# A decoder layer on one core: where the third expert weight piece lands, and which engine normalises the last layer norm's rows

## The reference

```python
x = x + _L0_attn_ref(_layernorm(x, axis=-1), Wq, Wk, Wv, Wo, betas)            # segmented attention with a memory, 16 heads
x = x + _L0_xattn_ref(_layernorm(x, axis=-1), ctx_512, Wq, Wkv_expand, Wout)   # cross attention, 16 heads of 16
x = x + _L0_ffn_ref(_layernorm(x, axis=-1), gate, w0, w1, wo)                  # 8 experts, the best 2 of each token

def _layernorm(x, axis=-1, eps=1e-05):
    m = jnp.mean(x, axis=axis, keepdims=True)
    v = jnp.var(x, axis=axis, keepdims=True)
    return (x - m) / jnp.sqrt(v + eps)
```

## Time and profile before

| | us |
|---|---|
| median of three executions | 536.52 (533.1 to 539.55) |
| the profiled execution's own time | 537.06 |
| its span, first to last instruction | 534.8 |
| attention, to the barrier | about 303 |
| cross attention | about 88 |
| experts and the end | about 144 |

### The profile page before, as it was taken

The page is one execution under the profiler, slowest core; times in us unless marked ns, Lnnn a source line. Parts: engine busy times, 40 slices in busy tenths (PEclk is TensorE's granted clock), DMA queues, the critical chain, the costliest instruction groups (busy, mean ns, idle before and its releaser), DMA issues. The chain is left out here.

```text
span 534.8 us, 11854 instructions
## 1 busy us (share of the span) xinstructions
PE 491.5 (92%) x4181; PEld 418.1 (78%) x4190; DVE 343.3 (64%) x743; ACT 318.4 (60%) x759; POOL 134.3 (25%) x150
## 2 busy tenths in 40 slices
PE   8899999999999999999999879999849999999970
PEld 3778888888898888888779857777637888888860
DVE  6666666667644676666558465678674667666754
ACT  4677777778526777777673267898313444544430
POOL 5710000012100000000000189996122433443220
PEclk9999999999999999999999997999859999999995
DMA  9521111211100112210000243441044555554527
GB/s 263 182 61 60 59 59 59 59 54 46 29 31 21 45 57 59 59 59 20 1 1 2 68 131 119 130 149 42 1 157 150 153 162 174 164 143 165 167 69 245
DMA packets 25043, 49.10 MB, mean 92 GB/s; under 512 B 2977, under 2 KB 12210, under 8 KB 25010
## 3 DMA queue, kind: packets, MB, share of 16 engines
q1 hardware_dynamic: 20434, 40.65, 25.0%
q0 software_dynamic: 2240, 6.04, 3.3%
q10 hardware_dynamic: 2336, 1.97, 1.2%
HBM read 42.48 MB, written 6.16 MB: 91 GB/s over the span
## 5 line engine op out<-in xcount | busy, mean ns | idle before, releaser
L717 PE MATMUL psum<-a_xt_hi,a_qk_hi 128*128 128x512 f32 x128 | 53.7, 420 | 0.9 <-POOL a_qk_lo L325 0.9
L629 DVE COPY a_weights_t<-psum 64x256 f32<-64x256 f32 x32 | 13.7, 428 | 60.7 <-PE psum L834 60.7
L717 PE MATMUL psum<-a_xt_hi,a_qk_lo 128*128 128x512 f32 x128 | 50.1, 392 | 0.0
L1066 ACT ACTIVATE x_probs<-psum,x_neg_max 128x128 f32<-128x128 f32 x128 | 45.8, 401 | 7.1 <-DVE x_neg_max L1124 7.1
L717 PE MATMUL psum<-a_xt_lo,a_qk_hi 128*128 128x512 f32 x128 | 50.0, 390 | 0.0
L1558 ACT ACTIVATE e_inner_hi<-psum 128x512 fp32r<-128x512 f32 x23 | 13.8, 598 | 56.4 <-PE psum L1734 56.4
L1002 POOL MEMSET x_v_pad<- 128x1024 f32 x1 | 1.0, 952 | 167.5 <-POOLq L262 167.5
L1723 PE MATMUL psum<-expert_w_hi,e_x_hi 128*128 x92 | 38.4, 418 | 1.2 <-ACT e_x_hi L1538 1.2
L1515 POOL DMA_INDIRECT picks_dram<-x_wout,e_pick_row x23 | 22.7, 987 | 62.6 <-DVE x_wout L1671 62.6
L1663 DVE TENSOR_TENSOR e_inner_lo<-psum,e_inner_hi 128x512 fp32r<-128x512 f32 x23 | 15.9, 692 | 34.6 <-ACT e_inner_hi L1558 34.6
L848 PE MATMUL psum<-a_weights_t,a_v 64*128 64x64 f32 x256 | 34.9, 276 | 3.5 <-issue 2.6
(11 more groups left out here) (235 smaller groups left out, 1497.6 us busy)
## 6 DMA issues: line engine op xcount, KB each, us to landing
x_k_t<-in_expert_wo SPq DMA_DIRECT2D x23, 512.0 KB, 3.8
a_qk_raw<-in_wqk SPq DMA_DIRECT2D x32, 256.0 KB, 2.6
x_xn_t<-in_expert_w SPq DMA_DIRECT2D x13, 512.0 KB, 3.8
a_wv_raw<-in_wv SPq DMA_DIRECT2D x17, 256.0 KB, 2.8
xn_dram<-xn SPq DMA_DIRECT2D x2, 1024.0 KB
x_probs_t<-in_expert_w SPq DMA_DIRECT2D x3, 512.0 KB, 3.8
x_sb<-in_x SPq DMA_DIRECT2D x2, 512.0 KB, 4.8
x_k_t<-in_wo SPq DMA_DIRECT2D x1, 1024.0 KB, 10.4
```

Source lines behind the costliest of these rows:

```text
L717: last = pe.matmul(out, pick_l(left[a], k), pick_r(right[b], k), start=start and n == 0, stop=n == 3 * KD - 1, skip_group_check=not start)
L1066: last = act.activation(probs[:, ch, place, :], s_ps[ch][:, place, :], ACT.Exp, bias=neg_max[:, ch, place:place + 1], accum_out=sums[:, b ...
```

## The change

Two things change in `cross_phase`.

First, EARLY goes from 3 to 2, and `xn_t` is laid out by halves of the query columns: half 0 holds both row blocks of the first 512 columns (pairs 0 and 1), half 1 the others. A raw piece lands in one half. Piece 2 goes to half 0 as soon as pairs 0 and 1 are projected (`q_done` = 2), piece 3 to half 1 when all four are (`q_done` = 4), and from piece 4 on a piece is requested when the one two before it is split. The first two copies of `copy_weights` wait for piece 0 (u = 0) and piece 1 (u = 1) only.

Second, the rows of the third layer norm of batches 0 to 6 are made by POOL behind piece 15, not by DVE; batch 7 stays on DVE. POOL's first `root_of` moves behind piece 15 too. Each row instruction on POOL waits for the scores that still read its part of `xn`.

```diff
-EARLY = 3
+EARLY = 2
-    xn_t = sb("x_xn_t", [P, KD, B * S], F32)
+    xn_t = sb("x_xn_t", [P, HALVES, KD, BANK], F32)
...
-                if n == EARLY:
-                    sp.wait_ge(q_done, B // 2)
-                if 2 <= n < EARLY or n >= EARLY + 2:
+                if n in (EARLY, EARLY + 1):
+                    sp.wait_ge(q_done, 2 * (n - EARLY + 1))
+                if n >= EARLY + 2:
                     sp.wait_ge(w_split, n - 1)
...
+            def layernorm(b):
+                if b <= HB:
+                    pool.wait_ge(rstd3_ready, with_deviation[b])
+
+                pool.wait_ge(s_done, min(2 * (2 * b + 2), 2 * B))
+                pool.tensor_scalar(c.xn[:, b, :], c.x_sb[:, b, :], c.meanvar[:, b, 0:1], c.rstd[:, b:b + 1],
+                                   ALU.subtract, ALU.mult).then_inc(xn3_ready, 1)
+
             for n in range(PIECES):
-                if n == PIECES - 1:
-                    root_of(0)
...
+            root_of(0)
+            for b in range(HB):
+                layernorm(b)
             root_of(1)
+            for b in range(HB, B - 1):
+                layernorm(b)
             root_of(2)
...
                 if u < 2:
-                    act.wait_ge(w_split, EARLY)
+                    act.wait_ge(w_split, u + 1)
...
-                    if b == B - 1:
-                        layernorm(0)
-                        layernorm(1)
...
-                if b == B - 1:
-                    layernorm(2)
...
                 if u < 2:
-                    dve.wait_ge(w_split, EARLY)
+                    dve.wait_ge(w_split, u + 1)
...
-            layernorm(3)
...
-            layernorm(4)
-            layernorm(5)
...
-            layernorm(6)
```

More of the change, by code:

```diff
@@ L965, in raw_piece @@
             return probs_t[:, n % 2, :, :].rearrange("p h t -> p (h t)")
-        return xn_t[:, n % 2, :]
+        return xn_t[:, n % 2, :, :].rearrange("p k t -> p (k t)")
     def piece_loaded(n):
@@ L1042, in _ @@
                     act.wait_ge(xt_done, 1)
-                act.activation(xn_t[:, 0, half * BANK:(half + 1) * BANK], c.bank[half * KD][:, :], ACT.Copy).then_inc(xt_low_ready, 1)
+                act.activation(xn_t[:, half, 0, :], c.bank[half * KD][:, :], ACT.Copy).then_inc(xt_low_ready, 1)
             act.wait_ge(consts, c.n_x_consts)
@@ L1103, in _ @@
                     dve.wait_ge(xt_done, 2)
-                dve.tensor_copy(xn_t[:, 1, half * BANK:(half + 1) * BANK], c.bank[half * KD + 1][:, :]).then_inc(xt_high_ready, 1)
+                dve.tensor_copy(xn_t[:, half, 1, :], c.bank[half * KD + 1][:, :]).then_inc(xt_high_ready, 1)
             dve.wait_ge(consts, c.n_x_consts)
@@ L1193, in layernorm @@
                 dve.wait_ge(rstd3_ready, with_deviation[b])
+                dve.wait_ge(xn3_ready, b)
                 dve.tensor_scalar(c.xn[:, b, :], c.x_sb[:, b, :], c.meanvar[:, b, 0:1], c.rstd[:, b:b + 1],
@@ L1245, in project_queries @@
                     for k in range(KD):
-                        last = pe.matmul(q_banks(pair)[i], wq[:, k, i * P:(i + 1) * P], xn_t[:, k, pair_tokens(pair)],
-                                         start=k == 0, stop=k == KD - 1)
+                        last = pe.matmul(q_banks(pair)[i], wq[:, k, i * P:(i + 1) * P],
+                                         xn_t[:, pair // 2, k, pair % 2 * 2 * S:(pair % 2 + 1) * 2 * S], start=k == 0, stop=k == KD - 1)
                 last.then_inc(q_done, 1)
```

## The result

The changed kernel took 533.9 us in the median (22 executions), the kernel before 539.3 beside it; the ratio is 0.994 (95%: 0.9914 to 0.9967). The medians are of all executions, and the ratio leaves out the slow ones of both kernels (four of these 22, one of them of 2606 us), so it isn't 533.9 / 539.3. In a second comparison the changed kernel took 533.88 us, and the ratio was 0.9921 (0.9881 to 0.9961). In microseconds of some 537 that is a gain of 3.2 (1.8 to 4.6) and 4.2 (2.1 to 6.4), where the prediction forecast 5.5 by its sum. So the gain is clear of noise and smaller than forecast; the median lies inside the range, 2.3 us above the forecast, and under 1% of gain was the case held likeliest.

What follows compares the result with a forecast made beforehand. The prediction took the start as bound by ACT's wait for POOL's subtraction and PE's slow clock behind it, the middle by ACT. Sum: 537.06 - 1.6 - 3.4 - 0.5 = 531.6 us, range 529.5 to 533.5.

Steps and rivals of the forecast that it cites:

- the case held likeliest: Whole execution: a time within about 1% (5.4 us) of the kernel before, given 0.59; faster 0.32, slower 0.09.
- The stall and the clock: Start of cross attention: ACT's copy of chunk 0 no longer waits 2.44 us for POOL, and PE's clock holds at 1.00.
- Both terms, 1.6 and 3.4 us: Chunk 2 starts 1.6 us sooner; chunk 2 to chunk 4 takes 7.67 us instead of 11.05 at full clock, 3.4 us.
- The rival that the clock falls all the same: At PE's short gap or in the scores and weighing after it: the 3.4 us are missing, 535.0 us; chance 0.11.
- Where POOL stands: Near the end of the pieces: POOL's first root, behind piece 15, ends at about 367.3 us.
- slack of 1.7 us: POOL's five waits for PE to have weighed a batch, 1.7 us in all, which were to vanish.
- The price of a row: One layer norm row instruction on POOL: 0.6 us taken by size, between 0.40 and 2.4 us.
- bound of 1.0 us: POOL's rows near the end: hidden from PE up to about 1.0 us an instruction.
- all are hidden: At 0.6 us each, POOL's rows 0 to 6 are done before PE asks for them, costing nothing.
- late-rows rival: Near the end: at 2.4 us a row on POOL, PE waits and the gain is lost, 538.2 us; chance 0.35.
- What DVE gains: Between reciprocal and last copy: without its rows there, DVE's copy comes sooner for PE's weighing of batch 7, 0.5 us.
- the third rival: Clock also holds near the end: weighing and four transposes gain 1.5 us more, 530.1 us; counted within the forecast's 0.52.

Runs made afterwards that it cites:

- filling the stall: Kernel before with 11 unread 128x256 matmuls added on PE behind chunk 2's scores, ACT's wait kept: 535.18 us, ratio 0.9956.
- the half rows: Changed kernel with POOL's seven row instructions over 128 columns instead of 256: 532.76 us, ratio 0.9907 to the kernel before.
- the epsilon version: Changed kernel with the epsilon of batches 0 to 3 added by POOL instead of DVE: 534.2 us, ratio 0.9949 to the kernel before.
- piece 15 behind four rows: Changed kernel with POOL's first root and rows of batches 0 to 3 ahead of piece 15: 534.98 us, ratio 0.9971 to the kernel before.
- piece 15 behind seven rows: Changed kernel with epsilon of batches 0 to 3 on POOL and piece 15 behind two roots and rows 0 to 6: 533.19 us, ratio 0.9897.

## Why the prediction was right or wrong

**The stall and the clock: right in every profile, to 0.1 us.** Copy at 315.66 us (315.73 forecast), chunk 2 at 318.45 (318.45), chunk 4 at 326.12 (326.1), clock 1.00. Both terms, 1.6 and 3.4 us, are there in every profile with the early piece; filling the stall showed the second by itself, at about 3.2 us (an estimate: 1.45 us gained at chunk 4 and 1.8 us of filling that came too long). The rival that the clock falls all the same is out.

**Where POOL stands: near, with the spread missed.** The root was put at 367.3 us, 63.9 us from the fill. It ended at 64.4, 65.7, 66.1 and 66.5 us in the profiles of the changed kernel, its second, the half rows and the epsilon version. The prediction took one landing time of 3.8 us from the page for each transfer; POOL has lost its slack of 1.7 us, so a late piece shifts all that follows.

**The price of a row: the step that failed.** 0.6 us was taken and 1.21 us measured, by the prediction's own bound of 1.0 us too much to be hidden. The sum put the rows' lateness at nothing ("all are hidden"); in its place PE waited 0.96 and 3.04 us for rows. The error in the working: between 0.40 and 2.4 us it took one value, by size, from an instruction of another kind. The rows nearest in form would have missed as far on the other side, for 1.21 us is twice 0.6 and half of 2.4: their slope of 8.6 ns a column was too steep, and between 0.364 us at 16 columns and 1.21 us at 256 it is 3.5 ns a column. Half a row at 0.78 us lies on that line (0.76). The late-rows rival was thus half right: PE waits for rows in each profile of the changed kernel, 0.96 and 3.04 us. It is not slower than before, since 2.2 us an instruction was the point for that.

**What DVE gains: looked at in the wrong place.** The sum held 0.5 us and looked at DVE's rows at their old place. It moved the loop by 5 us against POOL's pieces and didn't ask which of DVE's instructions would then stand beside POOL's. They were two: the addition of epsilon (0.7 us lost where it met a subtraction, nothing in the second profile) and, had the rows stayed, rows 0 and 1 (2.73 us in one profile and 3.5 in the other). Whether the two edits are worth more together than alone stays open: 0.9 and 0.6 us alone and 3.2 to 4.2 together by the medians, but 3.1, 2.1 and 5.1 us by the profiles.

**The sum against one execution.** The two profiles before took 537.06 and 536.85 us, the two after 530.45 and 531.36: 6.1 us apart, and the forecast of 531.6 us fits them. That is luck in part, and the medians gain 3.2 and 4.2 us. The profiles of the changed kernel are among its fastest executions: of those that the ratios compare, 9 of 29 have a mean granted clock above 0.9735 (one of 75 before), and the others lie 2 to 7 us higher. The mean clock rose from 0.9662 to 0.9705; with 0.4 to 0.5 us for each 0.001 among executions of one kernel, that is about 2 of the 3.4 us between the means (537.03 and 533.58 us).

What the slower ones lose isn't seen in a profile of the changed kernel. The profiles of its relatives show two forms. One is the clock falling near the end, at 375.5 and 376.1 us in two profiles with late rows (the epsilon version and the one with piece 15 behind four rows). The other has nothing to do with the change: low stretches in the attention, with the fill at 304.77, 306.32, 307.02, 312.53 and 312.63 us in five profiles, where the other eight have 303.3 to 303.7.

And the prediction took the 3.4 us of one profile as paid in every execution before, which their clocks speak against. In the 13 profiles the stretch at half clock behind the cross attention is at least 13.7 us long and the one at the end 11.9 us; with the 6.8 us at the start that makes a mean clock of at most 0.970 (an estimate from these lengths). Of the 75 executions before, 18 have 0.972 or more: 533.5 to 536.7 us, about 3 us less than the rest. If their other stretches are as in the profiles, the fall at the start is missing in them or shorter, and the change can't save there what the sum counts. How the shortfall divides among this, the late rows and the attention stays open.

**The clock near the end.** It held until the 383rd microsecond in both profiles of the changed kernel, as the third rival said; but it held in the second profile of the kernel before as well, so the change isn't shown to be the cause.

## What to carry over

When an edit moves one engine's loop against another's, lay both timelines over each other at the new offset and look for instructions that end together, also for those that nobody touched. A price that no row shows belongs in the sum with both bounds: here the guess by size and the one by form both missed 1.21 us by a factor of two. A stall of an engine can be worth itself plus the clock that it costs: in the profiles here 1.6 and 3.2 to 3.4 us. And before a term read from one profile goes into a sum for the median, compare the granted clocks of the other executions.

## What the runs showed of the hardware

A DVE TENSOR_SCALAR between tensors in SBUF can stand for as long as a POOL instruction on SBUF runs beside it: 4 columns took 2.16 us in place of 0.17, a row 2.50 in place of 0.40, each ending within 0.2 us of POOL's subtraction. An addition over a single column didn't, in the one place where it shows (0.15 us in the middle of a subtraction, in the version with piece 15 behind seven rows). DVE's copies out of PSUM didn't either: over the 13 profiles, 73 copies of 128x512 that lie wholly within a subtraction have a median of 0.69 us, as have the 89 that are clear of one. Such a wait shows as a long busy instruction and not as idle time, so a table of waits doesn't name it. The Trainium skill, SBUF — State Buffer, section Who interferes with whom, has this as an exclusive lock on a port pair that the two engines share, held for a whole instruction; copies, casts and tensor_scalar on VectorE can want it. For the additions of four columns and the rows the traces agree, with 2.16 and 2.50 us beside subtractions of 2.36 and 2.34.

A TENSOR_SCALAR with two operations and scalars for each partition costs 1.21 us at 128x256 on POOL, three times DVE's 0.40. The Trainium skill, GPSIMD Engine Reference, section Engine selection, calls one-input operations roughly line-rate; for this one the measurement differs, and decides.
